# Experts of a routed layer: from every expert on every token to blocks of 128 tokens sorted by expert

## Chip, cores and metric

The kernel runs on one NeuronCore of a Trainium2 chip. The metric is the device time of one execution in microseconds (us), taken as the median of several runs. Engines: PE (matrix products; PEld is its weight loads), DVE (vector), ACT (activation), POOL (GpSimd), SP (issues DMAs).

## The reference, cut to what matters

Four batches of 512 tokens of width 256 go through cross attention over 1601 keys with a two-layer network, then a routed layer of 8 experts (below), then a 16-head attention, then a layer of 64 small and 2 shared experts. Each part works on the normalised sum of what went before. Only the 8-expert layer is changed:

```python
logits = flat @ gate_w.T + gate_b
vals, idx = jax.lax.top_k(logits, 2)                    # 2 of 8 experts for each token
wts = jax.nn.softmax(vals, axis=-1)
t1 = jnp.einsum('td,efd->tef', flat, mlp1_w) + mlp1_b   # 256 -> 512, every expert
act = _swiglu(t1, 7.0)                                  # 512 -> 256
y = jnp.einsum('tei,edi->ted', act, mlp2_w) + mlp2_b    # 256 -> 256
out = jnp.sum(jnp.take_along_axis(y, idx[:, :, None], axis=1) * wts[:, :, None], axis=1)
return x + out
```

## The kernel before

The program has four stages on the same instruction streams: a (the first attention), m and b (its network and the 8 experts, written as one: `mb_pe`, `mb_act`, `mb_dve`, `mb_pool`), c (the 16-head attention, `w_pe` and its fellows; the mask of this input takes the branch "window") and d (the last layer). X[p, n, :] holds 16 tiles of 128 tokens, four to a batch. Engines wait for each other through semaphores alone, and each runs its list in the order written.

Stage m has MU = 8 units v (batch v // 2, half v % 2 of the hidden width). `m_hidden(v)` makes 512 hidden columns, `m_gelu` takes them out on ACT, POOL splits off the high half (`high_hidden`, L814), DVE the low half (`low_hidden`, L819), and `m_second(v)` multiplies back. PE does `m_hidden(v + 1)` ahead of `m_second(v)`. After a batch's second unit, `m_add` adds to X, `ln_moments`, `ln_rstd` (POOL, L298) and `ln_scale` (L308) give Z, `normalised_again` gives HZ (a second scaling, its power taken on POOL at L1156), POOL adds Z to X (L1159), and `ln_turn` (L319) transposes into ZT. `logits`, `turn_logits` and `two_greatest` find the two experts and weights; ACT's L1079 is a sigmoid.

Stage b has B_UNITS = 32 units, one for each expert e and batch b, in the order B_ORDER. Every float32 operand is held as two F32R parts, high and low, and `split_matmul` (L60 to L62) makes a product of three F32R products. A unit is

```python
b_hidden: 4 x 2 split products of 512 columns    # L60-L62, PS<-ZT,b_w, 24 instructions
b_second: 4 x 2 split products of 256 columns    # L60-L62, PS<-b_w,m_h, 24 instructions
b_add:    X += weight of the expert x result      # L1239, 4 instructions
```

A token that did not choose e gets the weight 0. SP loads each expert's weights (`load_weights`); ACT and POOL split them. Between the units `extra` places small work: `biases` (L1025, the chosen experts' second biases, with `turn_weights` L1017), the third normalisation of batches 0 and 1, and the `EARLY` weights and context of stage c. Then `both_paths` makes every engine read a flag out of SBUF into a register (`value_load`) and branch. In stage c a unit u is a pair of heads of one batch, 32 in all; `masked` (L2289) needs the window masks that POOL makes (L2245), and the third normalisation of batches 2 and 3 is placed in units 2 to 7.

## Time and profile before

| | us |
|---|---|
| median of 3 runs | 1713.02 (1711.29 to 1715.24) |
| profiled execution, whole | 1709.99 |
| its span, first to last instruction | 1708.2 |
| PE busy | 1635.3 (96%) |
| DVE busy | 1110.7 (65%) |
| ACT busy | 718.4 (42%) |
| POOL busy | 379.9 (22%) |

In a profile, L12 is line 12 of the kernel; `out<-in` are tiles by name. A matrix instruction is shown with the length from its start to its modelled end, and the next one starts before that end; its rate is read from start to start. A float32 product whose operands are not split shows two instructions in the trace (13 products of `attend` at L450 show x26).

### The profile page before, as it was taken

To read this page: it belongs to the slowest core of one execution; us is meant where nothing else is said; L and a number is where in the kernel's file an instruction comes from. 1 tells how busy PE (TensorE), PEld (TensorE's weight loads), DVE (VectorE), ACT (ScalarE), POOL (GpSimd) and SP (SyncE) were. 2 spreads that over 40 slices of the span, in tenths; PEclk is the share of its full clock that TensorE was granted. 3 is DMA by queue.
4 is the path that set the end of the run, shared out by engine and by line. 5 is a ranking of instruction groups with operands and counts; after the bars stand their busy time and mean duration, and the time that the engine had idled before them with its cause. 6 is when DMAs were issued, how large, how long until landed. Compare 5 with 4: busy or idle time off the path is not lost.

```text
span 1708.2 us, 26543 instructions
## 1 busy us (share of the span) xinstructions
PE 1635.3 (96%) x9810; PEld 1321.4 (77%) x9810; DVE 1110.7 (65%) x2483; ACT 718.4 (42%) x1459; POOL 379.9 (22%) x373
## 2 busy tenths in 40 slices
PE   4999999999999999899999999999999899999998
PEld 3888887887888888566666666666688799989997
DVE  5666554568766677677667667667556676666663
ACT  2323322224333333666666666667444222222221
POOL 2102001543355445200000000001122333322321
PEclk8999999999999999999999999999999999999999
DMA  7032010000011100100000000000001554444532
GB/s 261 1 97 96 1 58 20 20 19 1 20 50 57 37 11 6 37 11 1 11 7 23 11 20 1 26 1 1 30 25 36 141 131 114 114 111 109 116 89 67
DMA packets 56202, 84.97 MB, mean 50 GB/s; under 512 B 5431, under 2 KB 32133, under 8 KB 56069
## 3 DMA queue, kind: packets, MB, share of 16 engines
q1 hardware_dynamic: 56069, 83.22, 18.0%
q8 instruction: 81, 1.33, 0.3%
q14 instruction: 52, 0.43, 0.1%
HBM read 80.58 MB, written 2.62 MB: 49 GB/s over the span
## 4 chain that ended last, share of the span: by engine, by line
PE 87%; DVE 6%; issue 3%; ACT 2%; DMA 1%; POOL 1%; SPq 0%; DVEq 0%; ACTq 0%; POOLq 0%
PE PS L60 19%; PE PS L62 19%; PE PS L61 18%; PE PS L2094 6%; PE PS L2106 6%; PE PS L2082 5%; PE PS L450 4%; PE PS L963 3%; PE PS L2121 3%; PE PS L518 1%; PE PS L319 1%; ACT c_pr L2190 1%; DVE a_pt L724 1%; DMA d_wb<-wscratch 1%; DVE a_c L653 1%
## 5 line engine op out<-in xcount | busy, mean ns | idle before, releaser
L1477 ACT ACTIVATE d_hf<-PS,C 128x512 f32<-128x512 f32 x160 | 108.2, 688 | 269.9 <-PE PS L62 262.6
L2199 ACT ACTIVATE c_pt<-PS 100x512 f32<-100x512 f32 x256 | 138.8, 594 | 141.1 <-PE PS L2094 140.9
L814 POOL CAST d_h<-d_hf 128x512 fp32r<-128x512 f32 x160 | 125.6, 796 | 318.5 <-DVE d_hf L1559 252.5
L60 PE MATMUL PS<-d_w,d_h 128*128 128x256 f32 x640 | 185.1, 289 | 10.4 <-DVE X L1549 8.9
L61 PE MATMUL PS<-d_w,d_h 128*128 128x256 f32 x640 | 182.4, 285 | 0.0
L62 PE MATMUL PS<-d_w,d_h 128*128 128x256 f32 x640 | 182.3, 285 | 0.0
L2190 ACT ACTIVATE c_pr<-c_sm,c_mn 128x400 f32<-128x400 f32 x256 | 158.4, 625 | 26.7 <-DVE c_mn L2289 26.7
L2289 DVE CUSTOM_DVE_ANT_0 c_sm<-PS,c_mw 128x400 f32<-128x400 f32 x256 | 136.1, 569 | 25.9 <-PE PS L2082 22.6
L298 POOL TENSOR_TENSOR rs<-ve,halfneg 128x4 f32<-128x4 f32 x16 | 16.6, 1038 | 611.9 <-DVE ve L293 611.9
L1559 DVE TENSOR_TENSOR d_hf<-d_hf,d_wb 128x512 f32<-128x512 f32 x128 | 92.5, 734 | 70.5 <-ACT d_hf L1477 69.1
L2094 PE MATMUL PS<-ident,c_pr 128*100 128x128 f32 x1024 | 138.3, 278 | 0.0
L819 DVE TENSOR_TENSOR d_h<-d_hf,d_h 128x512 fp32r<-128x512 f32 x160 | 126.2, 844 | 13.6 <-POOL d_h L814 13.6
L60 PEld LDWEIGHTS PS<-d_w,d_h 128*128 128x128 f32 x640 | 123.6, 193 | 13.9 <-issue 12.0
L2094 PEld LDWEIGHTS PS<-ident,c_pr 128*100 128x100 f32 x1024 | 106.3, 128 | 34.8 <-issue 28.7
L60 PE MATMUL PS<-ZT,d_w 128*128 128x512 f32 x320 | 128.1, 400 | 1.8 <-issue 1.8
L61 PE MATMUL PS<-ZT,d_w 128*128 128x512 f32 x320 | 127.3, 398 | 0.0
L62 PE MATMUL PS<-ZT,d_w 128*128 128x512 f32 x320 | 127.1, 397 | 0.0
L61 PEld LDWEIGHTS PS<-d_w,d_h 128*128 128x128 f32 x640 | 124.0, 194 | 1.9
L2106 PE MATMUL PS<-c_pt,c_v 100*64 100x512 f32 x512 | 124.0, 605 | 0.0
L62 PEld LDWEIGHTS PS<-d_w,d_h 128*128 128x128 f32 x640 | 123.8, 194 | 0.0
L2082 PEld LDWEIGHTS PS<-c_k,c_q 64*128 64x128 f32 x768 | 61.5, 185 | 79.4 <-issue 70.5
L819 POOL TENSOR_TENSOR m_h<-m_hf,m_h 128x512 fp32r<-128x512 f32 x64 | 81.3, 1292 | 147.7 <-ACT m_h L812 147.7
(264 smaller groups left out, 3786.5 us busy)
## 6 DMA issues: line engine op xcount, KB each, us to landing
d_wb<-wscratch SPq DMA_DIRECT2D x64, 512.0 KB, 7.8
a_cT<-ctxT SPq DMA_DIRECT2D x4, 1601.0 KB, 6.6
a_nat<-ctx SPq DMA_DIRECT2D x4, 1536.0 KB
d_w1r<-l_w SPq DMA_DIRECT2D x10, 512.0 KB, 4.1
d_w2r<-l_w SPq DMA_DIRECT2D x10, 512.0 KB, 5.1
b_w1r<-mlp SPq DMA_DIRECT2D x8, 512.0 KB, 3.7
fl_m<-mask SPq DMA_DIRECT2D x4, 800.5 KB, 4.7
c_cr<-ctxT SPq DMA_DIRECT2D x8, 400.0 KB, 3.4
```

The source lines that it names most:

```text
L60: pe.matmul(out, w[0], x[0], start=first, stop=False)
L61: pe.matmul(out, w[0], x[1], start=False, stop=False)
L62: return pe.matmul(out, w[1], x[0], start=False, stop=last)
L814: i = eng.tensor_copy(mem["h"][b % 2][0][:, m, :], mem["hf"][:, m, :])
L819: eng.tensor_tensor(mem["h"][b % 2][1][:, m, :], mem["hf"][:, m, :], mem["h"][b % 2][0][:, m, :].bitcast(F32), ALU.subtract).then_inc(F["h ...
L1477: act.activation(memD["hf"][:, m, :], PS[:, m, :], ACT.Silu, bias=C[:, b1 + g * 4 + m:b1 + g * 4 + m + 1]).then_inc(DM["act"], 1)
L2082: last = pe.matmul(PS[:, BS + h, 0:WIN], c_q[u % 2][a][hs, i * P:(i + 1) * P], c_k[u % 2][c][hs, :], start=n == 0, stop=n == 2)
L2094: last = pe.transpose(PS[0:KW, BT + h, t * P:(t + 1) * P], c_pr[s % 3][h][:, t * KW:(t + 1) * KW], ident[:, :])
L2106: last = pe.matmul(PS[h * DH:(h + 1) * DH, BU, :], c_v[ph % 2][0:KW, t, p * P + h * DH:p * P + (h + 1) * DH], c_pt[u % 2][0:KW, h, t, :], ...
L2190: act.activation(c_pr[s % 3][h][:, :], c_sm[h][:, :], ACT.Exp, bias=c_mn[:, s % 4, h:h + 1], scale=-1.0, accum_out=c_l[:, s % 4, h:h + 1]) ...
L2199: act.activation(c_pt[u % 2][0:KW, h, :, i * P:(i + 1) * P], PS[0:KW, BT + h, :].rearrange("p (t q) -> p t q", q=P), ACT.Copy).then_inc(F[ ...
L2289: dve.tensor_tensor_reduce(c_sm[h][:, :], PS[:, BS + h, 0:WIN], c_mw[:, b * QT + i, :], 1.0, BIG, ALU.add, ALU.min, c_mn[:, s % 4, h:h + 1 ...
```

## The change

The two batches 0 and 1 form group 0, batches 2 and 3 group 1. For each group PE counts with small float32 products how many tokens chose each expert and each token's place in its expert's list (`count`, `places`, `blocks_table`); DVE turns this into the row numbers `e_at` and the expert of each of 23 blocks, `e_of`. POOL scatters the normalised rows (now `e_H`, all 16 tiles) with 16 indirect DMAs for a group, one for each tile and choice, into `zs`, a DRAM buffer of 23 x 128 rows filled with zeros beforehand. All 46 blocks are always run. SP loads blocks four at a time; for a block PE transposes the rows, multiplies them with the expert's weights, which lie whole and unsplit in SBUF and are addressed by a register, and adds the bias as a third product; DVE and ACT apply the gate; PE transposes back and multiplies with the second weights; ACT takes the result out, and SP stores it to `ys`. POOL gathers each batch's rows with 8 indirect DMAs, and DVE's `combine` adds them to X with their weights. Products of the blocks are unsplit float32. The semaphores BM and the splits of expert weights go. The diff, cut to its core:

```diff
+GR = 2
+GT = NT // GR
+NB = (GT * P * 2 + E0 * (P - 1)) // P
...
+        zs = [nc.dram_tensor(f"zs{g}", [NB * P, D], F32).ap() for g in range(GR)]
+        ys = [nc.dram_tensor(f"ys{g}", [NB * P, D], F32).ap() for g in range(GR)]
...
+        e_w1 = sb("e_w1", [P, E0, KD, 512])
+        e_w2 = sb("e_w2", [P, E0, 2, D])
...
+            for g in range(GR):
+                sp.dma_start(zs[g].rearrange("(n p) d -> p n d", p=P),
+                             e_zero[:, :].unsqueeze(1).to_broadcast([P, NB, D])).then_inc(SP_[f"z_in{g}"], 16)
...
+        BIAS_AT = [8, 11, 14, 17]
...
             for e in range(E0):
-                wait_past(sp, BM["w_lo"], e * 2)
-                load_weights(sp, BM, memB, mlp1, mlp2, e)
...
+                sp.dma_start(e_w1[:, e, :, :], mlp1[e].rearrange("(k p) n -> p k n", p=P)).then_inc(SP_["w_in"], 16)
+                sp.dma_start(e_w2[:, e, :, :], mlp2[e].rearrange("(k p) n -> p k n", p=P)).then_inc(SP_["w_in"], 16)
...
+            def load_chunk(c):
+                if c % NCH == 0:
+                    sp.wait_ge(SP_["moved0"], (c // NCH + 1) * 2 * GT * 16)
...
+                qs = chunk_blocks(c)
+                n0 = qs[0] % NB
+                sp.dma_start(e_z[c % 2][:, 0:len(qs), :],
+                             zs[c // NCH][n0 * P:(n0 + len(qs)) * P].rearrange("(n p) d -> p n d", p=P)
+                             ).then_inc(SP_[f"z_in{c % 2}"], 16)
...
+            for q in range(GR * NB):
+                for k, which, i in early_in(q + 1):
+                    if k == 0:
...
+                c, n = chunk_of(q)
+                if n == 0 and c + 2 < GR * NCH:
+                    load_chunk(c + 2)
+                sp.wait_ge(SP_["y_out"], q + 1)
+                sp.dma_start(ys[q // NB][q % NB * P:(q % NB + 1) * P], e_y[q % 2][:, :]).then_inc(SP_[f"stored{q % 2}"], 16)
+
...
+        def combine(dve, b):
...
+            dve.wait_ge(SP_[f"moved{b % 2}"], gathered(b))
...
+            for k in range(2):
...
+                for i in range(QT):
+                    t = b * QT + i
+                    dve.scalar_tensor_tensor(X[:, t, :], rows_of[:, k, i, :], e_wk[:, t, k:k + 1], X[:, t, :],
+                                             ALU.mult, ALU.add).then_inc(x_done[1], 1)
...
+        def gather(pool, b):
...
+            stored_until(pool, (b // 2 + 1) * NB)
+            if b == 3:
+                pool.wait_ge(x_done[1], 3 * 8)
...
+            for k in range(2):
+                for i in range(QT):
+                    at = e_at[:, b // 2, k, b % 2 * QT + i:b % 2 * QT + i + 1]
+                    pool.indirect_dma_start(rows_of[:, k, i, :], None, ys[b // 2][:, :],
+                                            bass.IndirectOffsetOnAxis(ap=at, axis=0)).then_inc(SP_[f"moved{b % 2}"], 16)
...
+            def count(g):
...
+                pe.wait_ge(BR["own"], (2 * g + 2) * OWN)
+                for t in range(GT):
+                    pe.matmul(PS[0:E0, 7, 0:1], e_own[2][:, g * GT + t, :], e_ones[:, 0:1], start=t == 0, stop=t == GT - 1)
+                pe.matmul(PS[:, 7, 64:64 + GT * E0], e_tri[:, :],
+                          e_own[2][:, g * GT:(g + 1) * GT, :].rearrange("p t e -> p (t e)"), start=True, stop=False,
+                          skip_group_check=True)
+                for t in range(GT - 1):
+                    for u in range(t + 1, GT):
+                        last = pe.matmul(PS[:, 7, 64 + u * E0:64 + (u + 1) * E0], e_ones[:, :], e_own[2][:, g * GT + t, :],
+                                         start=False, stop=False, skip_group_check=True)
...
+            def places(g):
...
+                pe.wait_ge(SP_["planned"], PLAN[g] + 4)
+                for t in range(GT):
+                    pe.matmul(PS[:, 7, 64 + t * E0:64 + (t + 1) * E0], e_nbB[:, :], e_tri[0:E0, 0:E0], start=False,
+                              stop=t == GT - 1, skip_group_check=True)
...
+            def turned(q):
...
+                for k in range(KD):
+                    last = pe.transpose(PS[:, 0, k * P:(k + 1) * P], e_z[c % 2][:, n, k * P:(k + 1) * P], ident[:, :])
+                last.then_inc(SP_["t"], 1)
+
...
+            def first(q):
...
+                expert[q] = pe.value_load(e_of[0:1, g, n:n + 1], min_val=0, max_val=E0 - 1)
+                w = e_w1[:, bass.ds(expert[q], 1), :, :]
...
+                pe.wait_ge(SP_["zt"], q + 1)
...
+                o = PS[:, 2 + q % 2, :]
+                for k in range(KD):
+                    pe.matmul(o, e_zt[q % 3][:, k, :], w[:, 0, k, :], start=k == 0, stop=False)
+                pe.matmul(o, e_hot[:, g, n:n + 1].to_broadcast([32 + E0, P]), e_b1[:, :], start=False, stop=True
+                          ).then_inc(SP_["h"], 1)
+
+            def turned_back(q):
+                pe.wait_ge(SP_["swiglu"], 3 * q + 3)
...
+                for k in range(2):
+                    last = pe.transpose(PS[:, 1, k * P:(k + 1) * P], e_h[q % 2][:, k * P:(k + 1) * P], ident[:, :])
+                last.then_inc(SP_["ht"], 1)
...
+            def second(q):
+                w = e_w2[:, bass.ds(expert[q], 1), :, :]
+                pe.wait_ge(SP_["ht_out"], q + 1)
...
+                for k in range(KD):
+                    last = pe.matmul(PS[:, 4 + q % 2, 0:D], e_ht[q % 2][:, k, :], w[:, 0, k, :], start=k == 0, stop=k == KD - 1)
...
+            pe.wait_ge(SP_["planned"], PLAN[0] + PL)
+            turns(2)
+            logits(2)
+            turn_logits(2)
+            pe.wait_ge(BR["own"], 3 * OWN)
+            turns(3)
+            turned(0)
+            turned(1)
+            first(0)
+            logits(3)
+            turned(2)
+            first(1)
+            turned_back(0)
+            for q in range(GR * NB):
+                if q + 3 < GR * NB:
+                    turned(q + 3)
+                if q + 2 < GR * NB:
+                    first(q + 2)
+                if q + 1 < GR * NB:
+                    turned_back(q + 1)
+                second(q)
+                tick(q)
 
         def mb_act(act):
...
+            def turned(q):
...
+                act.activation(e_zt[q % 3][:, :, :], PS[:, 0, 0:D].rearrange("p (k t) -> p k t", k=KD), ACT.Copy
+                               ).then_inc(SP_["zt"], 1)
+
+            def gate(q):
+                act.wait_ge(SP_["swiglu"], 3 * q + 1)
+                act.activation(e_gs[:, :], e_hf[:, 0:D], ACT.Silu, scale=ALPHA).then_inc(SP_["sig"], 1)
+
+            def out_of(q):
+                act.wait_ge(SP_["y"], q + 1)
+                wait_past(act, SP_[f"stored{q % 2}"], 16 * (q // 2))
+                act.activation(e_y[q % 2][:, :], PS[:, 4 + q % 2, 0:D], ACT.Copy).then_inc(SP_["y_out"], 1)
...
+        def scatter(pool, g, order):
...
+            for k, i in order:
+                pool.indirect_dma_start(zs[g][:, :], bass.IndirectOffsetOnAxis(ap=e_at[:, g, k, i:i + 1], axis=0),
+                                        e_H[:, g * GT + i, :], None).then_inc(SP_["moved0"], 16)
...
+            high(7, (0, 1))
+            scatter(pool, 0, ALL[0:2])
+            high(7, (2,))
+            scatter(pool, 0, ALL[2:4])
+            high(7, (3,))
+            ln_rstd(pool, 1, [2])
+            scatter(pool, 0, ALL[4:9])
+            rms(2)
+            scatter(pool, 0, ALL[9:])
+            z_add(2)
+            ln_rstd(pool, 1, [3])
+            rms(3)
+            z_add(3)
+            scatter(pool, 1, ALL)
+            for q in range(0, 24):
+                for k, which, i in early_in(q):
                     early_low(pool, k, which, i)
...
+            pool.wait_ge(SP_["moved0"], GR * 2 * GT * 16)
+            gather(pool, 0)
+            gather(pool, 1)
+            ln_rstd(pool, 2, [0])
...
+            def swiglu(q):
+                dve.wait_ge(SP_["h"], q + 1)
                 for j in range(2):
...
+                    dve.tensor_scalar(e_hf[:, j * D:(j + 1) * D], PS[:, 2 + q % 2, j * D:(j + 1) * D], float(j), LIMIT + j,
+                                      ALU.add, ALU.min).then_inc(SP_["swiglu"], 1)
+                dve.wait_ge(SP_["swiglu"], 3 * q + 2)
+                dve.wait_ge(SP_["sig"], q + 1)
...
+                dve.scalar_tensor_tensor(e_h[q % 2][:, :], e_hf[:, D:2 * D], 1.0 - LIMIT, e_gs[:, :],
+                                         ALU.max, ALU.mult).then_inc(SP_["swiglu"], 1)
+                dve.wait_ge(SP_["swiglu"], 3 * q + 3)
...
+            def back_out(q):
+                dve.wait_ge(SP_["ht"], q + 1)
...
+                dve.tensor_copy(e_ht[q % 2][:, :, :], PS[:, 1, 0:D].rearrange("p (k t) -> p k t", k=2)
+                                ).then_inc(SP_["ht_out"], 1)
...
+            def tick(q):
...
+                    two_greatest(3)
+                if q == 3:
+                    block_counts(1)
+                if q == 4:
+                    slots(1)
+                if q == 5:
+                    table(1)
+                if q == 6:
+                    routed(0)
+                    routed(1)
+                if q == 7:
+                    routed(2)
+                    routed(3)
+                for b in range(B):
...
+                for b in range(2):
+                    if q == 30 + 3 * b:
+                        combine(dve, b)
+                        ln_moments(dve, 2, [b])
+                    if q == (31, 35)[b]:
+                        ln_scale(dve, 2, b)
+                    if q == 33 + 4 * b:
+                        for j in range(2):
+                            ln_low(dve, 2, b, j, 6 + j)
...
-            pool.wait_ge(x_done[1], B_UNITS * QT)
...
+            pool.wait_ge(SP_["y_out"], GR * NB)
+            window_mask(0)
+            pool.wait_ge(PF["lo"], len(EARLY))
+            gather(pool, 2)
+            window_mask(1)
+            ln_rstd(pool, 2, [2])
+            gather(pool, 3)
+            add_bo(pool, 2)
+            window_mask(2)
+            window_mask(3)
...
-                                dve.wait_ge(x_done[1], B_UNITS * QT)
+                                combine(dve, b)
```

Of what the cut leaves out: `tables` makes constants on POOL in stage a, `biases_of_experts` prepares the first biases, `max_index` replaces `match_replace`, `EARLY` comes at blocks 15 to 35, `turn_weights` and `biases` at blocks 8, 11, 14, 17 and one after each, and batches 0 and 1 get `combine` and the third normalisation from block 30 on.

## Rows read from the trace of the kernel before

**Rows 1.** Stretches: length, busy us (count) of PE, PEld, DVE, ACT, POOL, clock, DMA share, GB/s.
```profile
370.60:672.60 302.00, 296.92 (x1695) 256.09 (x1695) 220.27 (x476) 113.69 (x185) 133.07 (x102) 0.99 0.08 25
672.60:1180.00 507.40, 492.79 (x3113) 327.60 (x3112) 351.96 (x1078) 339.55 (x845) 35.03 (x27) 1.00 0.04 13
```
**Rows 2.** The chain that ended last, the page's part 4.
```profile
PE 87%; DVE 6%; issue 3%; ACT 2%; DMA 1%; POOL 1%; SPq 0%; DVEq 0%; ACTq 0%; POOLq 0%
```
**Rows 3.** Timeline of PE in one expert unit: start us, us, instruction.
```profile
418.07 0.39 PE L61 MATMUL PS<-ZT,b_w 128*128 128x512 f32 x1
...
423.43 0.28 PE L60 MATMUL PS<-b_w,m_h 128*128 128x256 f32 x1
...
426.26 0.39 PE L60 MATMUL PS<-ZT,b_gate 128*8 128x512 f32 x1
```
**Rows 4.** Timeline of PE, float32 products and transposes in the two attentions.
```profile
21.68 1.84 PE L439 MATMUL PS<-a_bk,a_q 128*128 128x2 f32 x16
...
111.07 5.78 PE L450 MATMUL PS<-a_nat,a_pt 128*128 128x256 f32 x26
116.68 1.04 PE L518 MATMUL PS<-ident,a_p 128*128 128x128 f32 x8
...
806.70 1.94 PE L2106 MATMUL PS<-c_pt,c_v 100*64 100x512 f32 x8
```
**Rows 5.** The chain through the expert stretch: start us, us, what.
```profile
496.21 1.92 PE PS L1025 x8
...
543.01 0.44 PE PS L1017 x4
```
**Rows 6.** Groups by line and shape, DVE and ACT (busy us, mean ns, idle before).
```profile
L1239 DVE SCALAR_TENSOR_TENSOR X<-PS,b_wt,X 128x256 f32<-128x256 f32 x128 | 53.1, 477 | 26.4 <-PE PS L62 26.4
...
L287 DVE BATCH_NORM_STATS2 st<-X 128x6 f32<-128x256 f32 x64 | 22.4, 411 | 7.9 <-DMA X<-x 5.0 <-issue 2.8
...
L559 ACT ACTIVATE a_u<-PS 128x256 fp32r<-128x256 f32 x16 | 6.1, 383 | 0.2 <-PE PS L458 0.2
```
**Rows 7.** Timeline from the first layer's sixth unit on: PE, then DVE for batch 1.
```profile
350.80 5.92 PE L963 MATMUL PS<-m_w,m_h 128*128 128x256 f32 x48
...
349.77 0.41 DVE L1190 CUSTOM_DVE_ANT_0 zz<-Z 128x256 f32<-128x256 f32 x1
...
352.91 1.67 DVE L1197 SCALAR_TENSOR_TENSOR HZ<-Z,rs,R 128x256 f32<-128x256 f32 x4 [1.12 <-POOL rs L1156]
```
**Rows 8.** Groups by line and shape, POOL.
```profile
L814 POOL CAST m_h<-m_hf 128x512 fp32r<-128x512 f32 x32 | 22.2, 721 | 135.6 <-ACT m_hf L949 135.5
L298 POOL TENSOR_TENSOR rs<-ve,halfneg 128x4 f32<-128x4 f32 x16 | 16.6, 1038 | 611.9 <-DVE ve L293 611.9
...
L1159 POOL TENSOR_TENSOR X<-X,Z 128x1024 f32<-128x1024 f32 x4 | 9.6, 2400 | 7.1 <-DVE HZ L1197 7.1
```
**Rows 9.** DMA issues by line: KB each, median us from issue to landing.
```profile
b_w1r<-mlp SPq DMA_DIRECT2D x8, 512.0 KB, 3.7
```
**Rows 10.** Timeline over the reading of the flag and the branch into the attention.
```profile
672.49 0.28 PE L62 MATMUL PS<-b_w,m_h 128*128 128x256 f32 x1
672.61 0.40 PE L60 MATMUL PS<-c_wv,c_c 128*100 128x512 f32 x1
...
674.56 5.92 POOL L2245 TENSOR_SCALAR c_mw<-c_mu 128x400 bf16<-128x400 uint8 x5 [0.24 <-DVE X L1239]
```
**Rows 11.** Timeline, DVE's scaling beside a busy POOL and alone.
```profile
314.61 1.85 POOL L814 CAST m_h<-m_hf 128x512 fp32r<-128x512 f32 x3
314.68 2.24 DVE L308 TENSOR_SCALAR Z<-X,mv,rs 128x256 f32<-128x256 f32 x4 [1.13 <-POOL rs L298]
...
345.45 1.38 DVE L308 TENSOR_SCALAR Z<-X,mv,rs 128x256 f32<-128x256 f32 x4 [8.35 <-PE PS L319]
```
**Rows 12.** A stretch as in rows 1, and the timeline of PE at its start.
```profile
40.00:43.00 3.00, 3.00 (x13) 2.63 (x14) 0.83 (x2) 0.60 (x1) 0.00 (x0) 0.50 0.09 31
...
39.99 3.23 PE L518 MATMUL PS<-ident,a_p 128*128 128x128 f32 x13 [7.52 <-ACT a_p L590]
```

More of the change, by code:

```diff
@@ L10 @@
 I32 = mybir.dt.int32
+U32 = mybir.dt.uint32
 ACT = mybir.ActivationFunctionType
@@ L315, in ln_turn @@
             wait_past(pe, LN["lo"], q + 1 - freed)
-            src = HZ if rms else Z
+            src, at = (e_H, b * QT + 2 * j) if rms else (Z, 2 * j)
             for i in range(2):
@@ L1052, in mb_pe @@
             for v in range(MU):
                 if 1 <= v < MU - 1:
-                    m_hidden(pe, v + 1)
-                elif v == MU - 1:
-                    b_hidden(0)
-                m_second(v)
-                extra(v)
-            for n in range(B_UNITS):
-                if n + 1 < B_UNITS:
-                    b_hidden(n + 1)
-                b_second(n)
-                extra(MU + n)
+                    m_hidden(pe, v + 1, lambda half: m_tick(4 * v + half))
+                else:
+                    m_tick(4 * v)
+                    m_tick(4 * v + 1)
@@ new lines, in mb_act @@
+            m_gelu(act, 2)
+            act.wait_ge(BR["w_in"], 32)
+            act.activation(b_gate[0][:, :, :], b_gate_raw[:, :, :], ACT.Copy).then_inc(BR["w_hi"], 1)
+            for b in range(2):
+                m_gelu(act, 2 * b + 3)
+                high(b)
+                m_gelu(act, 2 * b + 4)
+                logits_out(b)
+                weights_of_two(b)
+            m_gelu(act, 7)
+            high(2)
+            logits_out(2)
+            weights_of_two(2)
+            high(3)
@@ L2382, in g_dve @@
             dve.wait_ge(PF["lo"], len(EARLY))
-            dve.wait_ge(x_done[1], B_UNITS * QT)
+            for b in range(2, B):
+                combine(dve, b)
             ln_dve(dve, 2, batches=range(2, B))
@@ L2389, in g_pool @@
         def g_pool(pool, m, F):
-            pool.wait_ge(x_done[1], B_UNITS * QT)
+            pool.wait_ge(PF["lo"], len(EARLY))
+            for b in range(2, B):
+                gather(pool, b)
             ln_rstd(pool, 2, range(2, B))
```

725 lines of the change are left out of this document (417 added, 308 removed).

## The prediction

> **What bounds the kernel now.** I read the busy time by stretch first. From the first expert product at 370.6 to the attention's first at 672.6 us PE is busy 296.9 of 302.0 us at a granted clock of 0.99, DVE 220, ACT 114, POOL 133 [rows 1]. The chain that ended last is PE's for 87% of the span [rows 2]. So PE sets the time of this stretch, and work taken off it counts in full until something else becomes late. The timeline then gives its rate. From the second instruction of a unit (418.07) to the first of the second half (423.43) are 23 steps in 5.36 us, 0.233 us for a split product of 512 columns; the next 24 steps take 2.83 us, 0.118 us for 256 columns [rows 3]. A unit is 24 x 0.233 + 24 x 0.118 = 8.4 us.
>
> **What goes.** 32 units, 32 x 8.4 = 269 us of PE. What is left of the 302 us is gate products, transposes, second biases and about 5 us idle, and it stays or is counted below.
>
> **What a block costs PE.** Unsplit float32 products are in the trace: 26 instructions, 13 products of 256 columns, from 111.07 to 116.68, 0.216 us each instruction, 0.43 us a product [rows 4]. For 512 columns, four products of L2106 (eight instructions) run in pairs in two halves of the array, 1.94 us with the last one's tail [rows 4], so at most 0.97 us for a pair, which is the time of one; twice the 256-column product is 0.86. I take 0.88. A transpose is 0.44/4 = 0.11 [rows 5]. A block is: two transposes 0.22, two first products 1.76 and the split bias product 0.23, two transposes back 0.22, two second products 0.87, and about 0.15 for changes between the kinds. Sum 3.45, taken as 3.5 us; 46 blocks, 161 us. All 46 always run, so what the tokens choose changes nothing.
>
> **Whether the others keep that pace.** DVE per block: two operations 128x256 out of PSUM, one with two SBUF inputs, one copy out of PSUM, each at most the 0.48 of L1239, which has both kinds of source [rows 6]: 1.9 us, 2.0 with waits on its own results. ACT: three of 0.38 [rows 6], 1.2 us. PE runs `turned` three blocks ahead, `first` two, so the chain from `first` over DVE and ACT and back (0.48 + 0.38 + 0.48 + waits, 1.6 us) lies under the next block's 3.5 us. A store of 128 KB lands within the 3.7 us of a load four times as large [rows 9] and has two blocks, 7 us. The four products with an address from a register and the register's load have no row. Below nothing they can't be. The one place where PE now reads a flag and branches shows no gap: its last expert product starts at 672.49, the next at 672.61; POOL shows 0.24 us at the same place [rows 10]. 
> **The start, where the new wait is.** PE no longer goes from the first network straight into experts; rows must be counted, scattered and read back. In the trace's own times: `m_second(5)` ends at 350.80 + 5.92 = 356.7 [rows 7]; gate products and transposes moved ahead of it add 2.7, 359.4. `count(0)` is 29 products with a 128-column stationary tile and 8 with a narrow one. Such an instruction takes 1.84/16 = 0.115 us [rows 4], float32 needs two: 29 x 0.23 + 1.0 = 7.7, so 367.1. Half of `m_hidden(7)` 2.8 and `places(0)` 8 x 0.23: 371.8. DVE's short chain of four tiny operations gives `e_at` at about 372.8, an estimate from below half of L1239's 0.48 each [rows 6]. Then POOL issues 16 scatters. An indirect DMA has no row. POOL's cheapest work is 0.72, its shortest arithmetic 1.04 us [rows 8]; the other end is one DMA for each landing, 3.7 us [rows 9]. I take 1.5, nearer to an instruction than to a landing, since nothing waits for each one. Between the scatters stand two casts 1.6, `ln_rstd` 1.0, `rms` 1.0: 24 + 3.6, so 400.4. Queued behind them are `z_add(2)` 2.4 and `ln_rstd` of batch 3 1.0 [rows 8]; DVE then scales (2.2 beside a busy POOL [rows 11]), squares (from 349.77 to 351.79, where the next operation begins to wait for POOL, 2.0), waits for POOL 1.1 and applies the result 1.7 [rows 7]: 410.8. PE stands in `turns(3)` until then, ahead of `turned(0)`; the first chunk, landed by 407, is not last. PE's list before was done at about 388, so some 23 us are idle. PE, idle for 7.5 us, ran the next 3 us at a granted 0.50, the lower of its levels, 1.2 GHz [rows 12]: 2 us for this restart.
>
> **The sum.** Start of the blocks 411; filling the pipeline 1.5; clock 2; blocks 161; `logits(3)` 1.8; `count(1)` and `places(1)` 9.8; second biases 4 x (1.92 + 0.45) = 9.5 [rows 5], there before too; 16 transposes for batches 0 and 1 1.8. DVE gets, for two batches, eight adds 3.3, moments 4 x 0.41 and a little [rows 6], scaling 2.2 [rows 11] and two subtractions 1.3 (twice L1239's width each), 2 x 8.8 = 17.6 us more, in blocks 30 to 37, where it has 8 x 1.5 spare, and about 10 in blocks 1 to 7: 8 us of stall. End 606.4 against 672.6, 66.2 us earlier. `gather(0)` starts when group 0 is stored, near block 25 (523), and its 8 DMAs are in by 537, before block 30. In the attention `combine(2)` and `combine(3)` add 6.6 us on DVE, of which I count 5 for PE, and `gather(3)`, which waits for `combine(2)`, has one unit of 15.9 us (507.4/32 [rows 1]) for 12 + 2.5 us: 1. Zeroing (5.9 MB) lies in the first attention, whose queue is mostly empty; at worst it delays one load, not counted. The window masks start where they did. Net -60: 1710.0 - 60 = 1650 for the execution profiled; the median of the runs shown lies 3.0 above it, so 1653 us.
>
> **The shared port.** DVE's four scalings took 2.24 us beside a busy POOL and 1.38 alone [rows 11], so the two already slow each other. The Trainium skill's page "SBUF — State Buffer" (Who interferes with whom) says the pair of ports is locked for a whole instruction, and that POOL can then not write DMA descriptors, 3.1 us where 0.62 were needed. By that the 16 scatters would cost about 16 x (3.1 - 1.5) = 26 us more; the row shows (2.24 - 1.38)/4 = 0.2 us an operation.
>
> **Rivals.**
> 1. *A scatter or gather costs 3 us on POOL.* For it: the landing rows; against: they queue. 16 x 1.5 = 24 later start, 12 of waiting for `gather(0)` and `gather(1)` at block 30, 10 for `gather(3)`: 1699. 0.20.
> 2. *Register reads are exposed at 0.24 us or a little more.* 1664; up to 1681. 0.10.
> 3. *Slower than before: PE cannot run ahead, and a block goes by its dependent path.* PE's list holds a register read and waits for DVE and ACT in each block; if each is met late, the path is transposes 0.22, ACT 0.4, products 2.0, gate 1.5, back 0.22, copy 0.5, products 0.87, about 5.7 us: 46 x 2.2 = 101, 1754. It decides from 3.5 + 60/46 = 4.8 us per block. Against it: the order two and three blocks ahead, and DVE's 2.0 us. 0.15 in all, with paces from 4 us on; 0.09 of it slower than before.
> 4. *Cheap scatters*, 0.7 us: 16 x 0.8 = 13 earlier and 7 from blocks at 3.35: 1633. 0.10.
> 5. The change can't fail to do what it says on the tensor side; a group's 23 blocks are fixed.
>
> **Numbers.** The forecast, 1638 to 1672, 0.45. The range 1630 to 1702 takes in rivals 1, 2 and 4 and leaves out the slow end of 3 and the tails. About 0.2% (3.4 us, the spread of the runs) is what a measurement can tell from no change. Faster: 0.45 + 0.20 + 0.10 + 0.10 + 0.04 = 0.89, less 0.02 for what no row names, 0.87; same 0.03; slower 0.10.
>
> **What will show it.** Per block 3.5 us between the starts of one block's first products and the next's; 46 x 2 float32 products of 512 columns; PE idle some 23 us from about 388 with POOL in scatters; `e_H` of batch 3 as the releaser of the first transposes; a clock of 0.5 right after; combines without long idle before them at block 30. Wrong would be: idle PE before each `first`, POOL over 2 us for a scatter, an attention stretch more than 10 us longer than 507, or a first stage made longer by the zeroing.

## The result, and the profile after

In the measurement made for the prediction the changed kernel took 1706.2 us (median of 6, 1703.2 to 1710.5) against 1713.9 us (1710.7 to 1718.0) for the kernel before: a ratio of 0.9957, 95% interval 0.9937 to 0.9978. Faster, as predicted, but by 7.6 us (under half a percent) and not by 60, and above the range (1630 to 1702). Four measurements of this same kernel were made in all, and they fall into two groups: 0.9957 and 0.9960 (1706.2, 1704.8), which I call the late group, and 0.9811 and 0.9803 (1680.1, 1679.4), the prompt group. So the miss from 1653 has two parts: 27 us that every execution shows, and some 26 us more that only the late group shows. Even the prompt group lies above the forecast's 1638 to 1672. I call the run of 1680.1 the second measurement and that of 1704.8 the fourth.

The stretches that answer to [rows 1]: first product of the blocks to the attention, and the attention to the last layer. First measurement, then second:

```profile
417.50:653.10 235.60, 209.76 (x763) 116.82 (x763) 101.22 (x286) 63.91 (x161) 51.79 (x47) 0.89 0.26 78
653.10:1209.40 556.30, 529.51 (x3307) 349.77 (x3305) 378.88 (x1147) 361.10 (x892) 52.56 (x43) 0.99 0.05 16
```
```profile
418.40:631.90 213.50, 202.52 (x763) 113.99 (x763) 102.92 (x286) 63.95 (x161) 51.99 (x47) 0.93 0.28 86
631.90:1183.80 551.90, 527.72 (x3306) 349.56 (x3305) 378.41 (x1147) 360.77 (x892) 52.59 (x43) 0.99 0.06 16
```

46 blocks at the predicted 3.5 us are 161 us, and all that stands between the first product and the attention was put at 193.9 (606.4 less 412.5); in the second measurement it took 213.5, at a mean clock of 0.93 where the kernel before had 0.99. The attention (to 1216.6 before, so 544.0 us) took 551.9.

A block in PE's timeline, first measurement:

```profile
426.73 1.88 PE L1189 MATMUL PS<-e_w,e_zt 128*128 x4
428.55 0.50 PE L1190 MATMUL PS<-e_b,e_hot 40*128 40x512 f32 x1
428.97 0.44 PE L1197 MATMUL PS<-ident,e_h 128*128 128x128 f32 x2
429.25 1.03 PE L1208 MATMUL PS<-e_w,e_ht 128*128 x4
430.11 0.38 PE L1170 MATMUL PS<-ident,e_z 128*128 128x128 f32 x2
430.33 1.88 PE L1189 MATMUL PS<-e_w,e_zt 128*128 x4
```

From start to start: first products 1.82 (predicted 1.76), bias 0.42 (0.23), transposes 0.28 and 0.22, second products 0.86; 3.60 us a block for the predicted 3.5. That step of the forecast holds but for 0.1 us.

Around the count of group 1 it does not look like that. The second measurement, PE's timeline:

```profile
442.72 8.38 PE L1108 MATMUL PS<-e_own,e_ones 128*128 128x8 f32 x56
450.95 0.67 PE L1170 MATMUL PS<-ident,e_z 128*128 128x128 f32 x2
451.41 3.62 PE L1189 MATMUL PS<-e_w,e_zt 128*128 x4
454.96 0.79 PE L1190 MATMUL PS<-e_b,e_hot 40*128 40x512 f32 x1
...
457.54 1.95 PE L1116 MATMUL PS<-e_tri,e_nbB 8*128 8x8 f32 x16
459.42 0.19 PE L1118 MATMUL PS<-e_nb,e_tri 8*8 8x1 f32 x2
459.54 0.44 PE L1170 MATMUL PS<-ident,e_z 128*128 128x128 f32 x2
459.81 3.02 PE L1189 MATMUL PS<-e_w,e_zt 128*128 x4
```

PE is never idle here, yet the same four instructions take 3.62 us in place of 1.88, and then 3.02: part of the stretch runs at the lower of its two clocks, 1.2 GHz (the mean granted clock from 442 to 463 is 0.69). What stands before is a run of 56 instructions with 8 moving columns. From the first products at 438.50 to those at 465.28 are 26.8 us for three blocks, 16.0 more than 3 x 3.60; the sum had 9.8.

What PE waited for between its first product and the attention, first and then second measurement:

```profile
PE PS L1197 <- DVE e_ht L1559: 12.6, 4, 5.4
PE PS L1170 <- ACT e_zt L1289: 7.2, 1, 7.2
PE PS L1138 <- ACT b_lt L1279: 3.8, 4, 0.9
```
```profile
PE PS L1197 <- DVE e_ht L1559: 7.2, 3, 4.4
PE PS L1138 <- ACT b_lt L1279: 3.8, 4, 0.9
```

### The profile page after: what moved, and what is told of

The parts are those of the page before. It is cut to its first block, busy times and chain, and to the rows that moved or that the text cites. A ratio compares the mean times of both kernels' runs of the same rounds, so it can differ in the third digit from the quotient of the medians.

```text
span 1701.5 us, 25269 instructions
## 1 busy us (share of the span) xinstructions
PE 1585.0 (93%) x9060; PEld 1208.9 (71%) x9060; DVE 1033.0 (61%) x2426; ACT 681.8 (40%) x1455; POOL 332.2 (20%) x357
## 4 chain that ended last, share of the span: by engine, by line
PE 53%; DVE 4%; issue 3%; ACT 2%; DMA 1%; another core or an unknown queue 0%; POOL 0%; SPq 0%; DVEq 0%; ACTq 0%; POOLq 0%
PE PS L67 11%; PE PS L69 10%; PE PS L68 10%; PE PS L2412 6%; PE PS L2424 5%; PE PS L2400 5%; PE PS L2439 3%; ACT c_pr L2508 1%; PE PS L1189 1%; DMA d_wb<-wscratch 1%; PE PS L1208 1%; DVE c_c L2592 0%; PE PS L1721 0%; DVE c_sm L2617 0%
## 5 line engine op out<-in xcount | busy, mean ns | idle before, releaser
L866 DVE TENSOR_TENSOR d_h<-d_hf,d_h 128x512 fp32r<-128x512 f32 x160 | 126.5, 847 | 12.6 <-POOL d_h L861 12.6
L2400 PE MATMUL PS<-c_k,c_q 64*128 64x400 f32 x768 | 106.0, 381 | 6.9 <-DVE c_mn L2617 6.9
```

What stands on the lines that cost most here:

```text
L866: eng.tensor_tensor(mem["h"][b % 2][1][:, m, :], mem["hf"][:, m, :], mem["h"][b % 2][0][:, m, :].bitcast(F32), ALU.subtract).then_inc(F["h ...
L2400: last = pe.matmul(PS[:, BS + h, 0:WIN], c_q[u % 2][a][hs, i * P:(i + 1) * P], c_k[u % 2][c][hs, :], start=n == 0, stop=n == 2)
```

## The experiments

Each ratio is to the kernel before on the same chip; times in us. They are grouped by what they test, not by order.

**The changed kernel again, three times.**

> The changed kernel once more, as it is. In its first profile the stores of the blocks landed up to 17 us after their issue while GpSimd issued 16 indirect DMAs, and PE was idle 7.2 and 7.8 us there. In all four experiments so far, two of which leave the stores and the indirect DMAs alone, a store landed in 1.7 us and neither stall is in the trace. Theory A (the four edits each removed it, by shifting when things meet): this run has the stalls again and takes about 1706. Theory B (the late stores belong to the chip or the process of that run, not to the kernel): no stalls; 15 us of idle PE and some 8 us of low clock less, 1680 to 1686, a ratio of 0.981 to the kernel before.

1680.1, ratio 0.9811 (0.9791 to 0.9832), as theory B had it.

> The changed kernel a third time, as it is. Its six executions of the first measurement took 1703 to 1710 us with two stalls of 7 to 8 us behind late stores, its five executions of the second 1679 to 1682 without them. Theory A (the late stores are a rare condition from outside the kernel): 1680 again, stores landed in 1.7 us. Theory B (either may come): 1706 with the stalls.

1679.4, 0.9803 (0.9777 to 0.9830).

> The changed kernel a fourth time, as it is, beside the next three. Of its first three measurements one had late stores and 1706.2 us, two had none and 1680.1 and 1679.4. Theory A (late stores are rare and from outside the kernel): 1680 again. Theory B: they come back, 1706.

1704.8, 0.9960 (0.9944 to 0.9977): theory B. This kernel and the three measured beside it ran on one chip, and all four are of the late group; the 14 profiles of the prompt group come from three other chips, one of them used twice. The chip of the first measurement is not on record. Since every late run but the first was made on that one chip at one time, the record doesn't separate the chip from the moment.

What is late? I first read it as the stores. ACT takes a block's result into one of two buffers, SP stores it, and the copy after the next needs the buffer again. SP's issue of a store in the fourth measurement, then ACT there, then ACT in the second:

```profile
464.78 0.32 SPq L998 DMA_DIRECT2D ys<-e_y  x1
...
468.25 0.39 ACT L1299 ACTIVATE e_y<-PS 128x256 f32<-128x256 f32 x1 [0.36 <-issue]
...
482.82 0.38 ACT L1299 ACTIVATE e_y<-PS 128x256 f32<-128x256 f32 x1 [6.11 <-remote]
483.10 0.38 ACT L1289 ACTIVATE e_zt<-PS 128x256 f32<-128x256 f32 x1
...
483.78 0.37 ACT L1299 ACTIVATE e_y<-PS 128x256 f32<-128x256 f32 x1
```
```profile
468.86 0.38 ACT L1299 ACTIVATE e_y<-PS 128x256 f32<-128x256 f32 x1 [0.36 <-PE PS L1208]
...
472.46 0.38 ACT L1299 ACTIVATE e_y<-PS 128x256 f32<-128x256 f32 x1 [0.29 <-PE PS L1208]
```

The copy at 482.82 needs the buffer whose store SP issued at 464.78, 18 us before. GpSimd's 16 scatters began at 460 and the last ended at 480.3. But two things in the same trace speak against a store that moves late. Its packets were moved at once: this is the DMA view of 464.7 to 467, where `q0` is GpSimd's queue and `q1` SP's.

```profile
q0 software_dynamic: 77, 0.18, 23.3%
q1 hardware_dynamic: 144, 0.13, 17.0%
ys<-e_y SPq DMA_DIRECT2D x1, 128.0 KB
```

The next store (468.66) has its 144 packets between 468.6 and 470.5 in the same way, and from 470.5 to 482.8 SP's queue moves nothing. And DVE is late too, where it waits for PE alone and for no store (`swiglu` waits for the block's bias product, L1190). Each pair is the product and DVE's first operation on it:

```profile
470.08 0.50 PE L1190 MATMUL PS<-e_b,e_hot 40*128 40x512 f32 x1
...
475.84 0.76 DVE L1545 TENSOR_SCALAR e_hf<-PS 128x256 f32<-128x256 f32 x2 [5.82 <-remote]
...
568.38 0.50 PE L1190 MATMUL PS<-e_b,e_hot 40*128 40x512 f32 x1
...
577.82 0.76 DVE L1545 TENSOR_SCALAR e_hf<-PS 128x256 f32<-128x256 f32 x2 [10.64 <-remote]
```

From one to the other are 5.8 and 9.4 us; in blocks without a stall they are 0.6. The second pair (block 28) is 7.3 to 9.9 us apart in all five profiles of the late group and under 1 us in the 14 others. So what the late group shows is that engines learn late that something is done, PE's products included, while 16 indirect DMAs are issued (460 to 480, and the gathers, 558.7 to 578.5). Whether the store's own signal is late as well the trace can't say: its packets are there, but some of its signals are missing from the record in this group, which is why these profiles give the stores no landing time (the prompt group's median is 1.7 us). PE waits 6.4 us at 474 and 7.5 us at 574, and restarts at the lower clock each time.

**Third buffer, and pauses between the indirect DMAs.** `e_y` three times (e3_third_y); the scatters of group 1 in pairs (e4_spaced), and with them the gathers of batches 0 and 1 (e15_paced):

```diff
+            for n in range(8):
+                pool.wait_ge(SP_["swiglu"], 3 * (6 + n))
+                scatter(pool, 1, ALL[2 * n:2 * n + 2])
```

> One more output buffer (three e_y tiles in place of two), so that a block's result waits for the store of the third block before it. In the changed kernel a store issued at 463.3 let ACT go on only at 480.1, and one issued at 563.4 only at 581.4, each time about when GpSimd's 16 indirect DMAs (459 to 479, 559 to 578) had ended; PE was idle 7.2 and 7.8 us there and ran the next block at the lower clock. Theory A (stores land late while indirect DMAs are being issued, and the two buffers turn this into a stall): with three buffers each stall shrinks by one block's time, 3.6 us, twice, and the blocks after it lose less clock: 8 to 12 us shorter, total about 1697. Rival B (the stall comes from the loads of the chunks or from GpSimd's lock on DVE's port): no change in the stalls.

1679.4, 0.9794 (0.9770 to 0.9819).

> The 16 scatters of group 1 are issued two at a time behind eight blocks (6 to 13), each pair waiting for its block's gate, in place of 16 without a pause. The gathers stay as they are. Theory A (a store lands only when the indirect DMAs issued before it have been worked off, so a pause lets it in): the 7.2 us of idle PE at 474.6 and the half clock behind it go, the stall in the gathers (7.8 us) stays; 9 us shorter, total about 1698. Rival B (each indirect DMA delays stores by a fixed share wherever it lies): the stall is split into several small ones with the same sum, no change in the total. Rival C (the stall is not from the indirect DMAs): it stays at its place.

1677.3, 0.9793 (0.9763 to 0.9823).

> The 16 scatters of group 1 and the 16 gathers of batches 0 and 1 are issued in pairs, each pair waiting for the gate of another block (blocks 6 to 13 and 26 to 33), so that GpSimd pauses 1.1 us in every 3.6 us. Nothing else is changed. The kernel of the change has been seen in two conditions: on some chips its stores land in 1.7 us also beside the indirect DMAs (1680 us), on others only when the run of indirect DMAs is over, after up to 18 us (1705 us). Theory A (on the slow ones a store waits for the software queue to run empty, and a pause is enough): on such a chip the stalls of 6.4 and 7.5 us go, 1682 to 1690; on the other kind 1676 to 1679, as with spaced scatters alone. Rival B (a store is late beside any indirect DMA, pauses or not, or the pauses are too short): on a slow chip 1700 or more, with stalls spread over more blocks.

1678.5, 0.9801 (0.9777 to 0.9825). All three fell into the prompt group, and they are that group's 1680 within 3 us: neither the buffer nor the pauses cost anything, and neither theory was tested, since there was no stall to remove. Whether they help in the late group remains untried. Their 27 us below the first measurement are not gains of the edits.

**The count of rows.** The 28 products that add earlier tiles' totals become 7 (and the 8 of `places` one):

```diff
-                for t in range(GT - 1):
-                    for u in range(t + 1, GT):
-                        last = pe.matmul(PS[:, 7, 64 + u * E0:64 + (u + 1) * E0], e_ones[:, :], e_own[2][:, g * GT + t, :],
...
+                for d in range(1, GT):
+                    last = pe.matmul(PS[:, 7, 64 + d * E0:64 + GT * E0], e_ones[:, :],
+                                     e_own[2][:, g * GT:(g + 1) * GT - d, :].rearrange("p t e -> p (t e)"),
...
```

> Both groups: the 28 products of 8 columns that make the prefix over tiles become 7 products of 56 to 8 columns with the same stationary matrix of ones, and the 8 products of places become one with a repeated moving operand. The same numbers are computed. In the changed kernel these stretches took 7.8 and 8.3 us (28 products each) and 2.0 us (8 products each), and in and behind the stretch in group 1 (442 to 463 us) the granted clock was 0.76 where the blocks before and behind it had 1.00. Theory A (many products of 8 columns cost their own time and leave TensorE at the lower clock for the next blocks): count falls to about 2 us, places to 0.3, and the first products after it stay at 1.88 us instead of 3.55 and 3.06; 2 x 8 us of products and about 5 us of clock, of which some at the start is lost because GpSimd's scatters set the pace there: the expert stretch 15 to 20 us shorter, total about 1688. Rival B (the clock fell for another reason, or the start is set by GpSimd alone): the products go, the clock in 442 to 463 stays under 0.85; 8 to 10 us shorter, total about 1697.

1661.3, 0.9692 (0.9667 to 0.9716), 18.8 less than the second measurement (on another chip; by the two ratios it is 20): theory A in full. The blocks start at 410.1 in place of 418.4, and behind the count nothing slows down:

```profile
434.29 1.68 PE L1107 MATMUL PS<-e_own,e_ones 128*128 128x56 f32 x14
435.82 0.41 PE L1170 MATMUL PS<-ident,e_z 128*128 128x128 f32 x2
436.07 1.88 PE L1189 MATMUL PS<-e_w,e_zt 128*128 x4
```

> Group 1 alone: the same 28 products of 8 columns as in the changed kernel, but placed 7, 6, 9 and 6 at a time behind four different blocks (3 to 6) instead of all behind block 3; places and the table follow three blocks later, the second biases one block later. Nothing is taken away. Theory A (it is the unbroken run of small products that lowers the clock): the blocks 3 to 8 all run at a granted clock of 1.0, first products 1.88 us each, and the stretch is about 5 us shorter; total about 1701. Rival B (the clock falls for another reason, or by the share of small products however they lie): some first products are still at 3 us or more, no gain beyond 1 us.

1675.0, 0.9771 (0.9740 to 0.9802), 5 less, though the two intervals touch; the clock is the better sign. This is the run that separates clock from work: all 28 products are there, and the stretch from 442 to 463 has a clock of 1.00, where the second measurement has 0.69; it falls only behind the undivided 16 instructions of `places` (second row):

```profile
442.00:463.00 21.00, 21.00 (x126) 14.58 (x123) 8.24 (x28) 4.98 (x13) 0.00 (x0) 1.00 0.16 51
463.00:470.00 7.00, 7.00 (x31) 4.04 (x30) 4.31 (x21) 1.01 (x4) 2.90 (x3) 0.76 0.38 131
```

**The register.**

> The register is taken out: each block uses expert n mod 8 (n the number of the block) with a fixed address, for both products; nothing reads the table of blocks on PE. What the block computes is so with the wrong expert, and the bias is still the routed one. The block's pace in the changed kernel is 3.60 us. Theory A (the register reads are covered, as the prediction took them): the pace stays 3.60, the same total as the changed kernel within 2 us. Rival B (they are exposed at 0.24 us or more a block): the pace falls to 3.36 or less, 11 us or more off the total.

1679.4, 0.9802 (0.9770 to 0.9833), against 1680.1 beside it; first products at 552.50 and 556.10, again 3.60 us apart. Theory A.

**The third normalisation in pieces.** `combine` takes one choice at a time; what stood in bundles from block 30 and from block 33 on stands in single pieces behind blocks 30 to 35 and 36 to 41.

> The third normalisation of batches 0 and 1 inside the blocks is cut into pieces of at most 1.8 us of DVE, one behind each block (adding the rows of the first choice, of the second, the moments, the scaling, the low halves), at blocks 30 to 41 in place of bundles of 5.6 and 6.4 us behind blocks 30 and 33. The same work. In the changed kernel PE waited 1.95 and 4.44 us for DVE's copy there, in both profiles that show it clearly, and ran part of the next block at a clock of 0.9. Theory A (the wait is the bundle ahead of the block's own gate): both waits go, 6 to 8 us shorter than the changed kernel unchanged in the same call. Rival B (DVE has no room for 17.6 us in blocks of 3.6 us, so the wait comes back in small pieces): 0 to 3 us.

1672.0, 0.9762 (0.9739 to 0.9785), 8.1 less, theory A. Of the 7.2 us of waits for DVE's copy only the one behind the last block is left:

```profile
PE PS L1140 <- ACT b_lt L1281: 3.8, 4, 0.9
PE PS L1199 <- DVE e_ht L1561: 0.8, 1, 0.8
```

**The second biases.** `biases(b)` two blocks behind `turn_weights(b)`, `BIAS_AT = [8, 12, 16, 20]`.

> The products of the second biases stand two blocks behind the transposes of the weights instead of one (and the four batches four blocks apart instead of three); the same work. In the changed kernel each of the four waited 0.94 us for ACT's copy of the transposed weights, which stands behind the block's own copy on ACT, and behind two of the four the next first products took 2.7 to 3.2 us at the lower clock. Theory A (the wait is one of order, and the gap with 8-row products is what lowers the clock): the 0.94 us waits go, 3.8 us, and with them one or two slow blocks of 1.6 us; 4 to 7 us shorter than the changed kernel in the same call. Rival B (the clock falls by the 8-row products alone): 3 to 4 us shorter, slow blocks as before.

1669.5, 0.9755 (0.9729 to 0.9781), 9.9 less than the third measurement's 1679.4 beside it, above both theories' sizes. Of this, 2.7 us lie in the start, which the edit does not touch (in the two profiles the blocks begin at 417.7 and 420.4), so that some 7 us are the edit's. The waits of 0.94 are gone, and so are all slow blocks behind the biases: the clock from 469 to 550 is 1.00.

```profile
469.00:550.00 81.00, 81.00 (x307) 45.77 (x308) 38.29 (x96) 28.60 (x72) 30.58 (x29) 1.00 0.42 129
```

The same 8-row products stand there, so rival B is out: they alone do not lower the clock. Something has to come with them: the idle 0.94 us before them, or the shorter distance between the four passes. The run changed both, so which of the two it is stays open.

> The second bias goes into the block: a third product of 256 columns with the same one-column selector as the first bias, its operand holding the eight second biases times 1.702 (the weights carry the inverse), split into a high and a low half. The four separate passes (transposes of the weights, ACT's copies, four products of 8 rows, two DVE additions a batch) go. The same result is computed. In the changed kernel a batch's pass cost 3.5 us of TensorE, once or twice with a slow block of 1.6 us behind it: 17 us for four. The added product: the first bias took 0.43 us for 512 columns from start to start; for 256 columns 0.2 to 0.3 us: 46 x 0.25 = 11.5 us. Theory A (the passes cost their time and the clock's dips behind them): 4 to 8 us shorter than the changed kernel in the same call. Rival B (the step to the next kind of product, not the columns, makes the 0.43 us, so the added one costs 0.4 us): 18 against 17 us, no change.

In the late group: 1705.5, 0.9955 (0.9936 to 0.9975), against 1704.8 beside it. Rival B. The block now takes 4.06 us, 0.46 more:

```profile
505.98 0.38 PE L1195 MATMUL PS<-e_b,e_hot 40*128 40x256 f32 x1
506.29 0.44 PE L1153 MATMUL PS<-ident,e_z 128*128 128x128 f32 x2
506.56 1.88 PE L1172 MATMUL PS<-e_w,e_zt 128*128 x4
```

The product itself takes 0.31 from start to start; the second products before it grow from 0.86 to 0.96, the transposes behind it from 0.22 to 0.27. 46 x 0.46 = 21 us replace 17.

**The start.**

> GpSimd's order in the gap before the blocks alone is changed: the power for batch 2 comes after 2 scatters instead of 5, batch 2's addition to X and batch 3's two powers come between the scatters instead of behind all 16. In the changed kernel batch 2's power was 3.2 us late and batch 3's 4.3 us, and PE stood idle 10.3 us before the first transposes (413.6), the last scatter ending at 404.5. Theory A (the normalisation of batch 3 sets the start, behind GpSimd's queue): the first product comes 3 to 5 us earlier, limited then by the last scatter and the load of the first chunk; 3 to 5 us off the total. Rival B (DVE's own chain or the clock sets it): under 1.5 us.

1682.0, 0.9817 (0.9793 to 0.9841): rival B. Batch 3's transposes came at 409.5 instead of 414.5, and PE then waited for the load, because the last scatter had moved from 405.4 to 412.5 (its end):

```profile
409.51 1.94 PE L360 MATMUL PS<-ident,e_H 128*128 128x128 f32 x8 [8.09 <-issue]
417.78 0.69 PE L1170 MATMUL PS<-ident,e_z 128*128 128x128 f32 x2 [6.33 <-DMA e_z<-zs]
```

**The attention.**

> In the stage of the 16-head attention the additions of the gathered rows of batches 2 and 3 to X are made for one column of 256 only (16 operations of DVE, left in their places with their waits); the result of these batches is so incomplete. The stage took 544.0 us in the kernel before and 553.5 in the changed one. Theory A (DVE's additions are the 9.5 us, as the prediction took for 5 of its 6): 16 x 0.4 = 6.6 us of DVE go, the stage falls to 547 to 549, the total by 5 to 7 us. Rival B (the gathers, batch 3's wait for batch 2's rows and the later second additions on GpSimd are it): the stage falls by less than 3 us.

This version leaves out most of the additions of batches 2 and 3, so its result is not the layer's. In the late group: 1699.3, 0.9913 (0.9884 to 0.9941). From the first product of the attention (652.2) to the last layer's (1203.7) 551.5 us, against 556.6 in the fourth measurement: 5.1 of the 12.6 that it had over the kernel before. Theory A is right in size; the other 7.5 stay unassigned (in the prompt group the whole surplus is 7.9, so some 3 if the additions cost the same).

**Together.**

> Three edits together: 7 wide products in place of the 28 narrow ones for both groups (1661.3 against 1680.1 for the changed kernel: 18.7 us), the third normalisation of batches 0 and 1 cut into pieces behind one block each (8.1 us), the second biases one block later (4 to 7 us expected). If each acts at its own place in the blocks, where TensorE sets the time, they add: 31 to 34 us, 1646 to 1649. If the clock's dips that one of them removes are made up for by another, less: about 1652.

1644.4, 0.9600 (0.9576 to 0.9625): 35.1 less than the changed kernel beside it; the parts sum to 36.8. They add. From its third block on the blocks without extra work step by 3.60.

> As the run with three edits, and GpSimd's order in the gap before the blocks changed only by half of what the earlier run did: batch 2's second power after 2 scatters instead of 5, its addition to X and batch 3's first power before the last four scatters. The earlier run brought batch 3's transposes 5 us forward, but its last scatter ended at 412.5 in place of 405.4 and PE then waited 6.3 us for the first chunk. Theory A (the start is the later of two chains, batch 3's rows and the last scatter with its load, and this order balances them): 1 to 3 us less than the run with three edits. Rival B (every microsecond taken from the one chain is added to the other, because GpSimd is busy without a pause): 0, or 1 to 2 us longer.

1642.9, 0.9589 (0.9566 to 0.9612), not told apart from the run before it; the blocks begin at 409.7 against 409.1, so the 1 to 3 us of theory A are not shown.

> The 7 wide products in place of 28 narrow ones, the third normalisation in pieces behind one block each, and the second bias as a third product of each block. If the edits add as before: 1680 - 18.7 - 8.1 and the gain of the bias in the block, 4 to 8 us: 1645 to 1649. The run with three edits that moved the biases instead took 1644.4; this one beats it only if the added product costs under 0.2 us.

In the late group: 1679.5, 0.9802 (0.9777 to 0.9827), 25.3 less than the changed kernel beside it; the stalls stay (PE waits 6.0 and 5.4 us).

> All that paid so far: 7 wide products for 28 narrow ones, the third normalisation in pieces, the second biases a block later, the balanced order on GpSimd at the start, three output buffers, and scatters of group 1 and gathers of batches 0 and 1 in pairs, paced by the blocks. Without the last two the same edits took 1642.9 us on a chip whose stores land in 1.7 us. Theory A (pacing and the third buffer cost nothing there and remove the late stores where they come): 1640 to 1645 on either kind of chip. Rival B (late stores stay): about 1643 on one kind, 1660 to 1668 on the other.

1643.6, 0.9583 (0.9556 to 0.9611), in the prompt group. There its two theories say the same, so the run doesn't decide between them. The version to keep is this one or e10's: both beat the kernel before by some 4.1%; neither has been measured in the late group.

## Why the prediction missed, step by step

Times are the second measurement's unless said otherwise; the predicted end of the blocks was 606.4, it was 631.9 (25.5 later) and 653.1 in the first.

- **What goes; pace of a block; register.** 3.60 for 3.5: 46 x 0.1 = 4.6 us. The bias product took 0.42 from start to start for the 0.23 read from a row where such products follow each other, and the other products 0.11 more than their terms; the 0.15 set aside for changes between kinds covers half of it. The register read costs nothing that can be seen (e5_const). The Trainium skill's floor of about 600 ns for it ("DMA: Bandwidth & Descriptors", Latency and other measured facts) is therefore either covered or does not bind here; the trace can't say which. Rivals 2 and 3 are out.
- **The start.** First products at 418.4 for 412.5. The first scatter began at 379.9 instead of 372.8: `count(0)` began 4 us late, and `m_hidden(7)` and `places(0)` ran at a clock of 0.55 to 0.68 behind it (first measurement, 368 to 382 us). A scatter cost 1.27 us for my 1.5 (0.96 and 0.30 to the next), which gave 3.7 back. So rival 1 is out, and so is rival 4's 0.7. The transposes of batch 3 began at 414.45 for 411, and from there to the first product, at the lower clock, were 4.0 us for 1.5 (the sum had 2 us for this clock in a term of its own, which is used up here and in the first block). PE's last wait was for batch 3, as said, with 10.2 us of idle time before it, though PE was idle for 16 us from 388 on and not for 23.
- **`count(1)` and `places(1)` 9.8.** A failing step of the part that all executions share: 16.0. Their own time is 11.1 (`count(1)` 9.0 for 7.7, `places(1)` and the table 2.1); the other 4.9 are the blocks behind them at the lower clock, which the sum put at nothing. [Rows 12] show that clock behind an idle stretch, and I looked for it nowhere else.
- **Second biases 9.5.** The largest failing step of the shared part: 17.2, four passes of 3.5 (0.94 of waiting for ACT and 0.43 of transposes beside the 2.0 of products) and twice a slow block of 1.6. The row of before [rows 5] gave the products, not what the order around them costs.
- **DVE's 8 us of stall.** 8.3 (6.4 of waiting, the rest a slow block behind it), and 1.7 of transposes. The mechanism is the predicted one, but the size is in part luck: the prediction's own figures give 17.6 - 12 = 5.6, and its 8 is not worked out. The stall is avoidable: the work fits if no piece is longer than a block's slack (e6_combine).
- **"Whether the others keep that pace."** The step that put the first measurement outside the range. It let DVE and ACT follow PE within 1.6 us and a store land within 3.7, also beside indirect DMAs; a scatter had a price on POOL only, and what it does to the others was put at nothing. In the late group two stalls of about 7 us each stood there (first measurement 7.2; then 1.1, 0.4 and 5.4), the lower clock behind each, and 4.4 us more in the attention. The kernel before has no indirect DMA, and none of its rows could show this. It is not the moving of the stores, whose packets are through within 2.3 us of their issue at the stalls of the late group too; DVE starts up to 9.4 us after PE's product in the fourth measurement. The Trainium skill ("DMA: Bandwidth & Descriptors", Queues, rings and completion order) has every DMA engine take turns between its queues packet by packet. The traces of both groups agree, as far as the packets of the two queues lie side by side (144 of SP's and 77 of GpSimd's from 464.7 to 467). Why the engines learn so late, and why only in some measurements, is open.
- **Attention +6.** +7.9, and +12.3 in the first measurement. Of this the additions of DVE, put at 5, are 5.1 (e14_thin).

Sum of the shared part: 5.9 + 4.6 + 6.2 + 7.7 + about 1 = 25.5, and 1.9 in the attention.

## What to carry to other kernels

Cost a run of narrow matrix products twice: for its own time, and for what comes behind it at the lower clock; make them few and wide, or lay them between dense work. Put side work on a second engine in pieces that fit one turn of the loop, and let what is made on one engine be used a turn later on the next. Measure a kernel with indirect DMAs several times, on more than one chip, before a verdict of a few per cent is believed. And before a late start is put down to a transfer, look whether its packets were late, and whether an engine that does not wait for it is late too.

## What the hardware showed that I had not expected

- TensorE fell to 1.2 GHz while it had not been idle at all: 56 instructions of 8 columns (8.4 us), then 3.62 us for what takes 1.88. The same 56 in runs of 12 to 18 between blocks left the granted clock at 1.00 (e2_spread).
- While GpSimd issued 16 indirect DMAs in a row, DVE began 7.3 to 9.9 us after the PE product that it waited for (block 28) in five profiles, four of them of one chip, and under 1 us after it in 14 profiles of three other chips. The packets of the stores at these stalls were moved within 2.3 us.
- An indirect DMA of 128 rows of 1 KB occupies GpSimd for 0.96 us, 1.27 from start to start. One of the first 16 took 2.61 while DVE made the low halves beside it (second measurement):

```profile
383.09 1.87 DVE L866 TENSOR_TENSOR m_h<-m_hf,m_h 128x512 fp32r<-128x512 f32 x3
...
383.21 2.61 POOL L1371 DMA_INDIRECT zs<-e_H,e_at  x1 [0.17 <-DVE e_of L1521]
...
386.12 0.97 POOL L1371 DMA_INDIRECT zs<-e_H,e_at  x1 [0.30 <-issue]
```

  From DVE's end (384.96) to the scatter's (385.82) are 0.86 us, about the length of an undisturbed one. The Trainium skill ("SBUF — State Buffer", Who interferes with whom) has GpSimd locked out of writing descriptors while DVE works in a two-port mode, and names `tensor_tensor` as an operation that did not stall DMAs. The length of this one scatter looks like the lock, but DVE's operation beside it is a TENSOR_TENSOR; the 15 others took 0.96 to 1.25.
- A split product of 256 columns put between unsplit ones costs 0.46 us a block; in [rows 3] such products in a row take 0.118 each.
